# A graph network's edge passes: stored target one-hots for two blocks of three, a four-deep ring of slot rows, and sums of three blocks in three PSUM banks

## The chip, the core and the metric

The kernel runs on one core of a Trainium2 chip. The metric is the time of one execution on the device in microseconds (us), taken several times; the profile is one further execution. "PE" is TensorE, "DVE" VectorE, "ACT" ScalarE, "POOL" GpSimd, and "SP" SyncE, which here only issues DMAs.

## The reference, cut to what matters

Four graph layers follow each other over 12500 nodes of 32 features and 212500 edges sorted by target. Each gathers rows of the source nodes, weighs them, and adds them up by target. The passes that the change touches do this three times:

```python
def prop(v):                                   # layer 1, called twice
    return jax.ops.segment_sum(w_hat[:, None] * v[src], dst, num_segments=n)
...
msg_sum = jax.ops.segment_sum(x[src], dst, num_segments=n)   # layer 3
```

The weight of an edge is folded in as `ew` per edge and a factor per node. Layer 3 has no weight.

## The kernel before, in words

There are five passes over the edges, called `s` = 0 to 4: layer 0 (s = 0), the two propagations of layer 1 (s = 1 and 2), the attention of layer 2 (s = 3) and layer 3 (s = 4). The change touches s = 1, 2 and 4, here pass 1, pass 2 and pass 4.

In these passes about half of the edges are handled in one way and half in another, side by side.

- **Groups.** A group is 1024 edges. POOL gathers its rows with eight indirect DMAs (L790) into one of four slots of `arena`. DVE weighs them (`weigh_group`, L1636) and compares the next group's targets (L2105), PE multiplies (`multiply_group`, L1190, into `ps_agg`), and DVE adds the 80-wide window to the sums (`add_group`, L1662), which sets the slot free (L1656) for the gather of four groups later.
- **Blocks.** A block is 4096 edges, sorted in pass 0 by source into 49 buckets of 256 nodes with 128 places each. A block is worked through in eight batches `q` of seven or six buckets. For a batch SP brings the low source numbers from `lows_d` to all partitions (L688), DVE makes one-hots of the sources (`compare_sources`, L1888), and PE picks the rows by matmul (`pick`, L1304, or L1301 in pass 2). In passes 1 and 2 DVE weighs the picked rows (L1941, L1944) and they are split into three bf16 parts: ACT copies the high part (L969), DVE forms the rest (L1953), ACT the middle part (L973), and DVE the low part (L1958). In pass 4 ACT casts the picked rows at once (L1000). The parts of a batch lie in `slot_rows`, a ring of two. PE then multiplies them with the one-hots of the targets (`send`, L1321) and sums the 49 buckets of a block in one PSUM bank, `ps_t` (`ps_agg` in pass 2), and DVE adds the bank to the sums in `big` (`add_block`, L1912, or three steps at L1908 in pass 2).
- **Target one-hots.** In pass 1 DVE makes them (`compare_targets`, L1898, 128x256 for a bucket) and SP stores them to `targets_d` in DRAM. In pass 2 SP reads them back (L706). Pass 4 has 39 blocks, in 13 turns of three; the first of a turn (`e` in `RETURNED`) takes stored one-hots, and DVE makes those of the second and third.

The order of the work is written out by hand: each engine has its own program, and a step of it handles several batches at once, shifted against each other (DVE weighs batch q, and takes the rest of q-1 and the low part of q-2). `HIDDEN` and `HIDDEN4` tell with which batch a group is handled. A pass 1 or 2 loop body is one block with four groups; a pass 4 body is one turn of three blocks and four groups. Waits are on semaphores that count: `s_sent` batches multiplied by `send` (it starts at 2), `s_sbadd` blocks added, `s_free` slots set free. Pass 2 also carries other work for the table of the attention pass (`build_piece`, `next_pair` and what belongs to them), on PE, ACT and ACT's DMA queue.

Two waits stand in the middle of the change. In step q ACT waits for `s_sent` before it writes the ring's entry, so that batch q-2 has been multiplied:

```python
act.wait_ge(s_sent, at + 1)
act.wait_ge(s_wgh, at + 1)
```

And PE's `send` of a block's first batch waits until the block before has been taken out of the bank:

```python
pe.wait_ge(s_sbadd, (BEFORE[h] + e + 1) + i * UNIT[s])
```

Of the kernel before, what the change touches and what calls it, by code (L numbers as in the profile page):

```python
# [19 lines left out]
BF16 = mybir.dt.bfloat16  # L20
# [4 lines left out]
P = 128  # L25
# [36 lines left out]
RETURNED = (0,)  # L62
# [54 lines left out]
def gnn_kernel(nc, x, src, dst, et16, et86, ew, ew1, w0, comp0, w1, b1, w2, comp2, selfw,  # L117
# [14 lines left out]
    with ctx:  # L132
# [86 lines left out]
        slot_rows = [m[:, 640:976].bitcast(BF16).rearrange("p (k c) -> p k c", c=SPLIT) for m in (mem_a, mem_b)]  # L219
# [100 lines left out]
        block_sums = {1: ps_t, 2: ps_agg, 4: ps_t}  # L320
# [526 lines left out]
        def _(act):  # L847
# [100 lines left out]
            def pick_and_lay_out(s, h):  # L948
# [8 lines left out]
                def pick_weighed(i, f, first, last):  # L957
# [4 lines left out]
                    for q in range(NBATCH + (9 if last else 0)):  # L962
                        at = ((BEFORE[h] + f) * NBATCH + q) + i * NBATCH
                        if q < NBATCH:
                            n, b = BATCHES[q][1], q % 2
                            act.wait_ge(s_sent, at + 1)
                            act.wait_ge(s_wgh, at + 1)
                            carry_wait(act)
                            nc.scalar.copy(slot_rows[b][:, 0:n, 0:D], by_tile(weighed[b][:, 0:n * D])).then_inc(s_high, 1)  # L969
                        if goes(q - 1):  # L970
                            n, b = BATCHES[(q - 1) % NBATCH][1], (q - 1) % 2
                            act.wait_ge(s_rest, at)
                            nc.scalar.copy(slot_rows[b][:, 0:n, D:2 * D], by_tile(rest[b][:, 0:n * D])).then_inc(s_mid, 1)  # L973
# [20 lines left out]
                def pick_block(i, e):  # L994
                    for q, (b0, n) in enumerate(BATCHES):
                        b, at = q % 2, ((BEFORE[h] + e) * NBATCH + q) + i * (UNIT[s] * NBATCH)
                        act.wait_ge(s_got, at + 3)
                        act.wait_ge(s_sent, at + 1)
                        carry_wait(act)
                        nc.scalar.copy(slot_rows[b][:, 0:n, :], picked_rows(b)[:, 0:n, 0:SPLIT]).then_inc(s_slot, 1)  # L1000
                        if q in HIDDEN4[e]:
                            lay_out_next(s, i, HIDDEN4[e][q])
# [183 lines left out]
        def _(pe):  # L1186
# [94 lines left out]
            def pick_and_sum(s, h):  # L1281
# [25 lines left out]
                def send(i, e, q):  # L1307
                    b0, n = BATCHES[q]
                    if q == 0:
                        pe.wait_ge(s_sbadd, (BEFORE[h] + e + 1) + i * UNIT[s])  # L1310
                        carry_wait(pe)
# [8 lines left out]
                    for k in range(n):  # L1320
                        last = nc.tensor.matmul(block_sums[s][0:SPLIT, 0:W2], slot_rows[q % 2][:, k, :], to_oh[s][q % TO_RING[s]][:, k, :],  # L1321
                                                start=(b0 + k == 0), stop=(b0 + k == NBK - 1))
# [261 lines left out]
        def _(dve):  # L1584
# [287 lines left out]
            def pick_and_sum(s, h):  # L1872
# [28 lines left out]
                def add_block(i, e):  # L1901
# [9 lines left out]
                    else:  # L1911
                        op = V.tensor_tensor(into, into, ps_t[0:SPLIT, 0:W2], ALU.add)  # L1912
# [6 lines left out]
                def pick_weighed(i, f, first, last):  # L1919
# [9 lines left out]
                    for q in range(NBATCH + ((8 if s == 2 else 4) if last else 0)):  # L1929
# [20 lines left out]
                        if goes(q - 1):  # L1950
# [3 lines left out]
                                            slot_rows[b][:, 0:n, 0:D], ALU.subtract).then_inc(s_rest, 1)  # L1954
                        if goes(q - 2):
                            n, b = BATCHES[(q - 2) % NBATCH][1], q % 2
                            dve.wait_ge(s_mid, count(i, f, q, -1))
                            V.tensor_tensor(slot_rows[b][:, 0:n, 2 * D:SPLIT], by_tile(rest[b][:, 0:n * D]),  # L1958
                                            slot_rows[b][:, 0:n, D:2 * D], ALU.subtract).then_inc(s_slot, 1)
                        if q % NBATCH == 2 and (q >= NBATCH or not first):  # L1960
                            add_block(i, f + q // NBATCH - 1)
                        if q - 3 in HIDDEN[s]:
                            add_group(s, i, HIDDEN[s][q - 3], f)
                        if q == 1 and not first:
                            add_group(s, i, SLOTS - 1, f - 1)
                        if q - 1 in HIDDEN[s]:
                            weigh_group(s, i, HIDDEN[s][q - 1], f=f)
                        else:
                            dve.drain()
# [7 lines left out]
                def pick_turn(i, f, first, last):  # L1977
                    for e in range(UNIT[s]):
# [5 lines left out]
                        for q in range(NBATCH):  # L1984
# [6 lines left out]
                            if q == 0 and not (first and e == 0):  # L1991
                                add_block(i, n - 1)
# [474 lines left out]
```

## Time and profile before

| | us |
|---|---|
| median of 3 runs | 7698.59 (7696.14 to 7699.79) |
| the profiled execution's own time | 7688.82 |
| its span in the trace | 7687.0 |
| pass 0 with its preparations | to about 2250 |
| pass 1, first to last group weighed | 2336.9 to 3411.2 |
| pass 2, first to last block added | 3524.2 to 4703.8 |
| attention (pass 3) | about 4790 to 6870 |
| pass 4, first to last block added | 6959.2 to 7639.1 |

Over the span PE is busy for 63%, DVE for 59%, ACT for 31% and POOL for 68%. These are averages over passes with different limits, so each pass has to be read by itself. In rows of a timeline the first number is the start and the second the duration in us, and the brackets give the idle time of the engine before and what ended it; "issue" is time for which the trace shows no releaser. The "us" of a wait is a sum over the stretch that was asked for, followed by how often and by the longest.

### The profile page before, as it was taken

The numbers are of one execution on the slowest core, as the hardware profiler recorded it, in microseconds if no ns is written. First come the engines' busy times: TensorE is split into PE (matmuls) and PEld (weight loads), VectorE is DVE, ScalarE is ACT, GpSimd is POOL, SyncE is SP. The second block draws the span as 40 slices with busy tenths as digits, with TensorE's granted clock in tenths as the row PEclk, the third lists the DMA queues.
The fourth block names the chain that finished last, engine by engine and source line by source line (L and its number), as shares of the span: only waits on it lengthen the run. The fifth ranks groups of instructions, "written<-read, shape, count | busy, mean of one in ns | idle before, by whom it ended". The sixth has DMA issues, their size and how long they took to land. (4 is left out here: it accounts for less than half of the span.)

```text
span 7687.0 us, 150121 instructions
## 1 busy us (share of the span) xinstructions
PE 4849.7 (63%) x41375; PEld 4128.6 (54%) x41376; DVE 4540.0 (59%) x14144; ACT 2349.6 (31%) x7420; POOL 5231.6 (68%) x5417
## 2 busy tenths in 40 slices
PE   5333333333336767776777775777777777786777
PEld 2222222222225555565666665777777777775667
DVE  5555555557778888875555553444444444447776
ACT  4444444440002222213545454111112111123222
POOL 2777777777756777757666662777777777756663
PEclk8655555555556666668888786555555555558998
DMA  7000000000004444436888887222222222216554
GB/s 173 14 14 14 14 14 14 14 14 13 13 12 122 128 128 126 129 103 189 293 276 293 272 293 231 41 41 41 41 41 41 41 41 41 41 34 162 154 162 116
DMA packets 539741, 757.13 MB, mean 98 GB/s; under 512 B 226073, under 2 KB 382265, under 8 KB 539509
## 3 DMA queue, kind: packets, MB, share of 16 engines
q1 hardware_dynamic: 309893, 395.03, 16.9%
q0 software_dynamic: 173168, 146.14, 12.1%
q10 hardware_dynamic: 56448, 213.62, 7.2%
q14 instruction: 179, 1.47, 0.1%
q8 instruction: 53, 0.87, 0.0%
HBM read 424.12 MB, written 330.21 MB: 98 GB/s over the span
## 5 line engine op out<-in xcount | busy, mean ns | idle before, releaser
L790 POOL DMA_INDIRECT arena<-table,ibuf x3328 | 3150.1, 947 | 1241.7 <-issue 1125.7
L790 POOL DMA_INDIRECT arena<-nodes,ibuf x2080 | 2078.8, 999 | 1070.7 <-issue 616.8
L1190 PE MATMUL ps_agg<-mem_a,arena 128*32 128x80 f32 (+1 forms) x3744 | 470.0, 307 | 555.6 <-DVEq L1643 506.9
L1190 PE MATMUL ps_agg<-mem_b,arena 128*32 128x80 f32 (+1 forms) x3744 | 473.5, 308 | 511.4 <-DVEq L1643 498.0
L1190 PEld LDWEIGHTS ps_agg<-mem_a,arena 128*32 128x32 f32 (+1 forms) x3744 | 411.2, 155 | 615.2 <-DVEq L1643 524.8
L1190 PEld LDWEIGHTS ps_agg<-mem_b,arena 128*32 128x32 f32 (+1 forms) x3744 | 413.8, 156 | 560.8 <-DVEq L1643 521.4
L1459 PE MATMUL ps_agg<-tbuf,msg 128*64 128x80 f32 x2496 | 373.6, 344 | 330.6 <-DVE msg L2128 330.6
L1061 ACT ACTIVATE att<-score 128x8 f32<-128x8 f32 x208 | 43.3, 208 | 1649.5 <-DVE score L2119 1649.5
L1459 PEld LDWEIGHTS ps_agg<-tbuf,msg 128*64 128x64 f32 x2496 | 336.1, 227 | 351.7 <-DVE msg L2128 351.7
L913 ACT ACTIVATE tbuf<-O,tbuf 128x49 bf16<-128x49 bf16 x1664 | 448.7, 363 | 79.2 <-DVE H L1810 79.2
L1888 DVE TENSOR_SCALAR tbuf<-idx_a,pcol 128x768 bf16<-128x768 bf16 (+1 forms) x1040 | 397.3, 425 | 109.5 <-issue 53.6
L2111 DVE TENSOR_TENSOR msg<-arena,ps_z 128x256 f32<-128x256 f32 x208 | 87.7, 421 | 554.4 <-DMA arena<-table,ibuf 554.4
L1636 DVE TENSOR_TENSOR arena<-arena,ew_s 128x256 f32<-128x256 f32 x416 | 178.0, 428 | 370.7 <-DMA arena<-table,ibuf 290.3
L1662 DVE TENSOR_TENSOR big<-big,ps_agg 32x80 f32 (+1 forms) x468 | 108.2, 231 | 485.7 <-PE ps_agg L1190 419.0
L1454 PE MATMUL ps_wide<-yw,mem_b 80*128 80x33 f32 x1680 | 380.6, 404 | 1.2 <-ACT yw L1043 1.2
L1454 PE MATMUL ps_h<-yw,mem_b 80*128 80x33 f32 x1664 | 377.0, 403 | 0.0
L1454 PEld LDWEIGHTS ps_wide<-yw,mem_b 80*128 80x128 f32 x1680 | 366.4, 331 | 19.0 <-issue 17.7
L1454 PEld LDWEIGHTS ps_h<-yw,mem_b 80*128 80x128 f32 x1664 | 362.9, 331 | 17.8 <-issue 17.8
L969 ACT CAST mem_a<-msg 128x224 bf16<-128x224 f32 x208 | 74.5, 358 | 878.4 <-PE ps_t L1321 522.9
L904 ACT COPY ibuf<-idx_a 128x8 int32 x208 | 39.7, 196 | 926.7 <-DMA arena<-table,ibuf 924.8
L1212 PE MATMUL ps_wide<-O,not_before 128*128 128x392 bf16 x156 | 82.3, 527 | 359.8 <-DVE H L1810 359.8
L1446 PE MATMUL ps_wide<-ident,tbuf 128*80 128x128 f32 x1248 | 297.7, 421 | 0.0
(392 smaller groups left out, 12081.6 us busy)
## 6 DMA issues: line engine op xcount, KB each, us to landing
table<-tbuf ACTq DMA_DIRECT2D x294, 544.5 KB
idx_a<-lows_d SPq DMA_DIRECT2D x637, 192.0 KB
targets_d<-tbuf SPq DMA_DIRECT2D x182, 384.0 KB
H<-targets_d SPq DMA_DIRECT2D x182, 384.0 KB
arena<-table,ibuf POOLq DMA_INDIRECT x3328, 2.5
table<-tbuf ACTq DMA_DIRECT2D x98, 495.0 KB
O<-targets_d SPq DMA_DIRECT2D x91, 384.0 KB
arena<-nodes,ibuf POOLq DMA_INDIRECT x2080
```

Source lines behind the costliest of these rows:

```text
L790: nc.gpsimd.indirect_dma_start(out=INTO[s][:, k, c, 0:WIDTH[s]], out_offset=None, in_=TABLE[s], in_offset=bass.IndirectOffsetOnAxis(ap=ibu ...
L913: op = nc.scalar.mul(moved[:, j, 2 + part, :], by_bucket[:, j, :], of)
L969: nc.scalar.copy(slot_rows[b][:, 0:n, 0:D], by_tile(weighed[b][:, 0:n * D])).then_inc(s_high, 1)
L1190: last = nc.tensor.matmul(ps_agg[ROW0[s]:ROW0[s] + CHN[s], 0:WIN], narrow[:, k, c, 0:CHN[s]], onehots[b][:, c, :], start=(c == 0), stop=(c ...
L1212: nc.tensor.matmul(ps_wide[:, r, 0:392], not_before[:, :], bucket_oh[:, at], start=True, stop=False)
L1446: nc.tensor.transpose(ps_wide[0:WIN, c // 4, (c % 4) * P:(c % 4 + 1) * P], rows[:, c, :], ident[:, :])
L1454: last = nc.tensor.matmul(y_own[b][:, c, :], onehot_t[:, c, :], yw[:, :], start=True, stop=True)
L1459: last = nc.tensor.matmul(ps_agg[0:2 * D, 0:WIN], msg[:, c, :], onehots3[k][:, c, :], start=(c == 0), stop=(c == CH - 1))
L1636: V.tensor_tensor(rows, rows, by[:, of].unsqueeze(2).to_broadcast([P, CH, D]), ALU.mult)
L1662: V.tensor_tensor(into, into, ps_agg[r0:r1, 0:WIN], ALU.add)
L1888: op = V.tensor_scalar(from_oh[s][q % 2][:, a, 0:n * CAP], lows[q % RING][:, 0:n * CAP], pcol2[:, a:a + 1], None, ALU.is_equal)
L2111: V.tensor_tensor(msg[:, :, D:2 * D], gbuf[:, k, :, PAIR:PAIR + D], last_in_ps.unsqueeze(2).to_broadcast([P, CH, D]), ALU.mult)
```

## The change: what it does

There are four parts.

1. Pass 4: `RETURNED` becomes (0, 1). Of a turn's three blocks the first two take stored target one-hots and DVE makes those of the third alone. SP issues eight more transfers in a turn, and DVE 49 comparisons (L1898) less.
2. Passes 1, 2 and 4: `slot_rows` becomes a ring of four. ACT waits for batch q-4 to have been multiplied where it waited for batch q-2.
3. Pass 4: successive blocks are summed in `ps_t`, `ps_z` and `ps_h` by turns; PE's wait before a block's first batch asks for the block three before, and DVE adds a finished block at batch 2 of the next one instead of batch 0.
4. Pass 1: DVE weighs a group (odd steps) and adds it one step later (even steps), where it added it two steps later, right before it weighed the next; the add stands ahead of `add_block`, and steps without a group lose their closing drain. Pass 2 keeps its order.

```diff
-RETURNED = (0,)
+RETURNED = (0, 1)
...
+        more_rows = sb("more_rows", [P, 576])
+        slot_rows = [m.bitcast(BF16).rearrange("p (k c) -> p k c", c=SPLIT)
+                     for m in (mem_a[:, 640:976], mem_b[:, 640:928], more_rows[:, 0:288], more_rows[:, 288:576])]
...
-        block_sums = {1: ps_t, 2: ps_agg, 4: ps_t}
+        block_sums = {1: [ps_t], 2: [ps_agg], 4: [ps_t, ps_z, ps_h]}
...
-                            act.wait_ge(s_sent, at + 1)
+                            if (BEFORE[h] + f) * NBATCH + q > 1:
+                                act.wait_ge(s_sent, at - 1)
...
-                        act.wait_ge(s_sent, at + 1)
+                        act.wait_ge(s_sent, at - 1)
...
-                        pe.wait_ge(s_sbadd, (BEFORE[h] + e + 1) + i * UNIT[s])
+                        pe.wait_ge(s_sbadd, (BEFORE[h] + e + 2 - len(block_sums[s])) + i * UNIT[s])
...
+                        if s == 1:
+                            if q - 1 in HIDDEN[s]:
+                                weigh_group(s, i, HIDDEN[s][q - 1], f=f)
+                            if q - 2 in HIDDEN[s]:
+                                add_group(s, i, HIDDEN[s][q - 2], f)
+                            if q == 0 and not first:
+                                add_group(s, i, SLOTS - 1, f - 1)
                         if q % NBATCH == 2 and (q >= NBATCH or not first):
                             add_block(i, f + q // NBATCH - 1)
...
-                            if q == 0 and not (first and e == 0):
+                            if q == 2 and not (first and e == 0):
                                 add_block(i, n - 1)
```

Every other use of `slot_rows[b]` becomes `slot_rows[q % 4]` (or q-1, q-2), and `add_block` reads the block's own bank.

DVE's program in the loop of pass 1, an odd step and the even step behind it. Before, L1953 and L1958 end the split of a batch, L1662 is the add of a group, L1636 the weighing and L2105 the comparison for the next group:

```order
L1953 TENSOR_TENSOR msg<-msg,mem_a 128x192
L1958 TENSOR_TENSOR mem_b<-msg,mem_b 128x6x32
...
L1662 TENSOR_TENSOR big<-big,ps_agg 32x80
...
L1636 TENSOR_TENSOR arena<-arena,ew_s 128x8x32
L2105 ISA
L2105 TENSOR_TENSOR mem_a<-iota,drel 128x640
L1888 TENSOR_SCALAR tbuf<-idx_a,pcol 128x768 x2
```

Of the changed kernel, in the same place (its lines are L1956, L1961, L1639, L2116, L1891, L1665 for the same six; the add stands at the end):

```order
L1956 TENSOR_TENSOR msg<-msg,more_rows 128x192
L1961 TENSOR_TENSOR mem_b<-msg,mem_b 128x6x32
L1639 REGISTER_ALU
L1639 TENSOR_TENSOR arena<-arena,ew_s 128x8x32
L2116 ISA
L2116 TENSOR_TENSOR mem_a<-iota,drel 128x640
L1891 TENSOR_SCALAR tbuf<-idx_a,pcol 128x768 x2
...
L1901 TENSOR_SCALAR tbuf<-iota,at_f 128x256 x6
...
L1665 TENSOR_TENSOR big<-big,ps_agg 32x80
```

The add has moved from ahead of the weighing to the end of the next step.

DVE's program of pass 4 around the start of a turn's second block. Before, the target one-hots (L1898) are made into `O` and the finished block is added from `ps_t` at once:

```order
L1888 TENSOR_SCALAR tbuf<-idx_a,pcol 128x768 x2
L1898 TENSOR_SCALAR O<-iota,at_f 128x256 x7
L1902 ISA
L1902 TENSOR_LOAD block_i
L1912 ISA
L1912 TENSOR_TENSOR big<-big,ps_t 96x256
L2105 ISA
L2105 TENSOR_TENSOR mem_a<-iota,drel 128x640
```

Of the changed kernel, from the start of a turn on (L1891 compares sources, L1915 adds the block before, which lies in a bank of its own):

```order
L1891 TENSOR_SCALAR tbuf<-idx_a,pcol 128x768 x2
L1905 ISA
L1905 TENSOR_LOAD block_i
L1915 ISA
L1915 TENSOR_TENSOR big<-big,ps_h 96x256
L1635 ISA
L2116 ISA
L2116 TENSOR_TENSOR mem_b<-iota,drel 128x640
```

In the first two blocks of a turn the rows of L1901 (the former L1898) are gone, and the add comes behind three comparisons of sources.

## Rows read from the trace of the kernel before

**Rows 1.** Busy time by engine (x instructions), PE clock, DMA share, GB/s, by pass

```profile
2330.00:3420.00 1090.00, 780.44 (x6015) 642.93 (x6015) 926.58 (x2885) 241.03 (x1044) 825.04 (x827) 0.66 0.45 127
3480.00:4710.00 1230.00, 919.72 (x13928) 785.15 (x13928) 657.07 (x1992) 602.70 (x1844) 796.84 (x822) 0.81 0.85 274
6959.00:7640.00 681.00, 499.75 (x6386) 436.70 (x6383) 533.65 (x2052) 201.20 (x353) 414.85 (x391) 0.95 0.58 155
```

**Rows 2.** Waits in pass 1, 2400 to 3400: us in total, times, longest

```profile
POOL arena L790 <- issue: 223.5, 733, 0.3
POOL arena L790 <- DVEq L1656: 10.1, 33, 0.3
```

**Rows 3.** Timeline of pass 1, an even and an odd step

```profile
2852.89 2.34 PE L1190 MATMUL ps_agg<-mem_b,arena 128*32 128x80 f32 x16
...
2854.52 0.35 DVE L1958 TENSOR_TENSOR mem_a<-msg,mem_a 128x192 bf16<-128x192 f32 x1
2855.11 0.76 DVE L1888 TENSOR_SCALAR tbuf<-idx_a,pcol 128x768 bf16<-128x768 bf16 x2 [0.24 <-issue]
...
2859.15 0.23 DVE L1662 TENSOR_TENSOR big<-big,ps_agg 32x80 f32 x1
2859.64 0.42 DVE L1636 TENSOR_TENSOR arena<-arena,ew_s 128x256 f32<-128x256 f32 x1 [0.27 <-issue]
```

**Rows 4.** Timeline of pass 4, an add that waits for PE

```profile
7219.24 1.29 PE L1190 MATMUL ps_agg<-mem_a,arena 128*32 128x80 f32 x16
...
7220.76 0.23 DVE L1662 TENSOR_TENSOR big<-big,ps_agg 32x80 f32 x1 [2.47 <-PE ps_agg L1190]
```

**Rows 5.** Waits in pass 2, 3600 to 4600

```profile
ACT mem_a L969 <- PE ps_agg L1321: 243.2, 81, 7.1
...
DVE msg L1953 <- ACT mem_a L969: 129.3, 44, 3.8
...
DVE msg L1953 <- ACT mem_b L969: 50.7, 51, 2.8
```

**Rows 6.** L1908, three for each block of pass 2: ns, first and last start

```profile
L1908 DVE TENSOR_TENSOR big<-big,ps_agg x78: 415/419/424, 3524.2 to 4703.8; 32x256 f32 x78
```

**Rows 7.** Timeline of pass 2, one step

```profile
4002.36 2.34 PE L1190 MATMUL ps_agg<-mem_b,arena 128*32 128x80 f32 x16 [0.30 <-issue]
4004.63 1.27 PE L1321 MATMUL ps_agg<-H,mem_a 128*96 128x256 bf16 x6
...
4006.04 0.35 ACT L969 CAST mem_a<-msg 128x192 bf16<-128x192 f32 x1 [3.32 <-PE ps_agg L1321]
...
4006.43 0.36 DVE L1953 TENSOR_TENSOR msg<-msg,mem_a 128x192 f32<-128x192 f32 x1 [3.28 <-ACT mem_a L969]
...
4007.40 0.24 DVE L1662 TENSOR_TENSOR big<-big,ps_agg 32x80 f32 x1 [0.35 <-issue]
```

**Rows 8.** L1912, one for each block of pass 4

```profile
L1912 DVE TENSOR_TENSOR big<-big,ps_t x39: 401/410/420, 6959.2 to 7639.2; 96x256 f32 x39
```

**Rows 9.** Stretches of pass 4: two busy moments, and a block with made one-hots

```profile
7208.00:7210.00 2.00, 0.43 (x4) 0.17 (x2) 0.13 (x1) 0.03 (x1) 1.39 (x3) 1.00 0.99 281
...
7280.00:7282.00 2.00, 1.01 (x19) 0.88 (x18) 1.11 (x5) 1.12 (x3) 1.56 (x2) 1.00 1.01 374
...
7228.26:7246.82 18.56, 13.98 (x184) 11.87 (x181) 17.49 (x72) 5.68 (x10) 13.86 (x12) 1.00 0.40 98
```

**Rows 10.** Timeline of DVE at the start of a turn of pass 4

```profile
7209.87 0.89 DVE L1888 TENSOR_SCALAR tbuf<-idx_a,pcol 128x768 bf16<-128x768 bf16 x2 [2.42 <-issue]
7213.75 0.42 DVE L1912 TENSOR_TENSOR big<-big,ps_t 96x256 f32 x1 [3.00 <-issue]
```

**Rows 11.** Instruction queue, packets and MB: 7000 to 7600, then 2400 to 3400

```profile
q14 instruction: 53, 0.43, 0.2%
...
q14 instruction: 3, 0.02, 0.0%
```

**Rows 12.** PE's wait for stored one-hots in pass 4, 7000 to 7600

```profile
PE ps_t L1321 <- DMA O<-targets_d: 5.9, 10, 0.8
```

More of the change, by code:

```diff
@@ L1320, in send @@
                     for k in range(n):
-                        last = nc.tensor.matmul(block_sums[s][0:SPLIT, 0:W2], slot_rows[q % 2][:, k, :], to_oh[s][q % TO_RING[s]][:, k, :],
+                        last = nc.tensor.matmul(block_sums[s][e % len(block_sums[s])][0:SPLIT, 0:W2], slot_rows[q % 4][:, k, :], to_oh[s][q % TO_RING[s]][:, k, :],
                                                 start=(b0 + k == 0), stop=(b0 + k == NBK - 1))
@@ L1911, in add_block @@
                     else:
-                        op = V.tensor_tensor(into, into, ps_t[0:SPLIT, 0:W2], ALU.add)
+                        op = V.tensor_tensor(into, into, block_sums[s][e % len(block_sums[s])][0:SPLIT, 0:W2], ALU.add)
                     op.then_inc(s_sbadd, 1)
@@ L1957, in pick_weighed @@
                             dve.wait_ge(s_mid, count(i, f, q, -1))
-                            V.tensor_tensor(slot_rows[b][:, 0:n, 2 * D:SPLIT], by_tile(rest[b][:, 0:n * D]),
-                                            slot_rows[b][:, 0:n, D:2 * D], ALU.subtract).then_inc(s_slot, 1)
+                            V.tensor_tensor(slot_rows[(q - 2) % 4][:, 0:n, 2 * D:SPLIT], by_tile(rest[b][:, 0:n * D]),
+                                            slot_rows[(q - 2) % 4][:, 0:n, D:2 * D], ALU.subtract).then_inc(s_slot, 1)
+                        if s == 1:
[5 more added lines that the diff above has]
+                                add_group(s, i, SLOTS - 1, f - 1)
                         if q % NBATCH == 2 and (q >= NBATCH or not first):
                             add_block(i, f + q // NBATCH - 1)
[L1962 to L1969, printed above, removed]
+                        if s == 2:
+                            if q - 3 in HIDDEN[s]:
+                                add_group(s, i, HIDDEN[s][q - 3], f)
+                            if q == 1 and not first:
+                                add_group(s, i, SLOTS - 1, f - 1)
+                            if q - 1 in HIDDEN[s]:
+                                weigh_group(s, i, HIDDEN[s][q - 1], f=f)
+                            else:
+                                dve.drain()
                         if s == 2 and q % 4 == 2 and (q >= 6 or not first) and q < NBATCH + 4:
```

9 lines of the change are left out of this document (4 added, 5 removed).

## The prediction

> **What bounds the kernel now.** I split the span by pass first, because its averages mix stages with different limits [rows 1]. Pass 1 is tight twice: DVE is busy for 926.58 of 1090 us, and POOL for 825.04, in 827 gathers of 0.998 us. The waits of pass 1 add what the busy time hides [rows 2]: POOL pauses about 0.30 us ahead of every gather and never longer than 0.3 us, so it never waits for a slot. 32 gathers for a block at 0.998 + 0.30 give 41.5 us, and pass 1 takes about that for a block. No wait of DVE there is for another engine or a DMA either. Both are full, DVE in its own order, and freeing slots earlier can bring POOL nothing.
>
> Pass 2 takes (4703.8 - 3524.2) / 25 = 47.2 us for a block [rows 6], and nothing is full: DVE 53%, PE 75%, ACT 49%, DMA 0.85 [rows 1]. Its waits form a loop [rows 5]: ACT waits for PE's `send` (243.2 us in 1000), DVE for ACT's high part (129.3 + 50.7), and PE's next batch for DVE. One step shows it link by link [rows 7]: `send` ends at 4005.90, ACT starts the high part at 4006.04, DVE goes on at 4006.43 after 3.28 us.
>
> Pass 4 takes (7639.1 - 6959.2) / 38 = 17.89 us for a block, 53.7 us for a turn [rows 8]. A block whose one-hots are made takes 18.56 us with DVE busy for 17.49 of it [rows 9]: DVE bounds it. At a turn's start DVE stands still twice with no releaser, 2.42 and 3.00 us [rows 10], while PE has nothing to do.
>
> **Part 1, stored one-hots for the second block (pass 4).** It takes 49 comparisons from a DVE that is the bound there, and puts 49 x 64 KB = 3.21 MB on the DMA engines. What the block costs then is the DMA's: its one-hots and 1.61 MB of source numbers are 4.82 MB. I price this in two ways. By bytes: in the five stretches of 2 us from 7200 to 7300 in which the share was 0.92 or more, the rate was 281 to 374 GB/s, 321 on average [rows 9]; 4.82 MB take 15.0 us. By share: a turn has 0.58 x 53.7 = 31.1 us of DMA time [rows 1], a made block 0.40 x 18.56 = 7.4 [rows 9], so the returned block has 31.1 - 2 x 7.4 = 16.3 us. I take 15.7. Two such blocks in a row are 31.4 us, less the two batches that SP fetches ahead while the third block leaves the DMA idle (0.79 MB, 2.5 us); with the made block, which stays at DVE's 18.56, the turn is 31.4 - 2.5 + 18.6 = 47.5 us. The saving is 6.2 x 13 = 81 us. The ends: no turn can be shorter than its 32 gathers, 41.5 us by pass 1's pace (157 us saved); and if the engines get no fuller than pass 2's 0.85, the block by share costs 16.3 / 0.87 = 18.8 us, the turn 53.7, and nothing is saved. I take no loss here from the two fetched blocks alone; what could make one is the last rival.
>
> **The standing still at the turn's start (pass 4).** The instruction queue moved 53 packets of 8 KB in 600 us of pass 4 and 3 in 1000 us of pass 1 [rows 11]: about four for each turn. DVE's loop of pass 4 is the longest of the three (336 instructions in the built program, against 283 and 299 in passes 1 and 2), and the change cuts it to 287. I expect the two pauses to vanish. They are not added to the 81 us, since the DMA goes on fetching during them and it is the DMA that sets the new turn.
>
> The Trainium skill ("Runtime: NRT & Kernel Launch", Instruction fetch mechanics) says that a taken branch to a target outside a window of two pages of 256 instructions has to fetch before it goes on. By that rule the pauses of rows 10 are the loop's jump back, and where a loop lies matters as much as its length: loops shift in the changed program, and one that comes to span three pages would pay at each turn. The trace agrees as far as the four packets go.
>
> **Part 3, three PSUM banks (pass 4).** PE no longer waits for `add_block`, 0.5 us after a block's end in the made ones. In the returned blocks the DMA hides it; in the made one DVE is the bound and still does the same add. I count 0.
>
> **Part 2, the ring of four.** In pass 1 DVE has no wait for ACT at all, and in pass 4 ACT hardly waits for `send`: 0. In pass 2 it opens the loop. DVE's waits for the high part are 180 us in 1000, 8.5 us for a block [rows 5]. Not all comes back. In the step of rows 7 DVE would take up L1953 about 2.7 us earlier, but its add of the group then waits for PE's L1190, which ends at 4004.70, so the add starts near 4004.9 instead of 4007.40: 2.5 us for DVE. PE, which is back to back behind it, gains only the 0.9 us or so that it waited for ACT. A gain between 0.9 and 2.5 of 3.28 is 27 to 76%, 2.3 to 6.5 us for a block. What comes next is near: POOL's 32 gathers take 32 x (0.969 + 0.30) = 40.6 us [rows 1], and DMA goes from 0.85 to 0.91 when a block falls to 44. I take 3.0 us, close to the low end, because PE is the slower partner: block 44.2, and 3.0 x 25 = 75 us. The ends are 0, since a wait is loosened and nothing is added, and 6.2 x 25 = 155, at 41.0.
>
> The Trainium skill ("DMA: Bandwidth & Descriptors", Specifications) gives about 358 GB/s as a core's share of HBM. Pass 2 moves 274 GB/s of it [rows 1], so by that rule its block could not fall under 36 us, which changes nothing; a returned block of pass 4 would take 13.5 us and the turn 43.3, a saving of 135 us. The trace reaches that rate in one of the five stretches and lies under it in four.
>
> **Part 4, the new order in pass 1.** It moves the add of a group to the end of an even step, and there PE has only just multiplied. L1190 ends at 2855.23, DVE's L1958 at 2854.87 [rows 3]; over the 104 groups the middle value of that lag is 0.31 us. DVE starts 0.23 us after PE has ended [rows 4]. So the add begins about 0.54 us after L1958. Summing the pauses of two steps from rows 3: before, 0.24 (L1958 to L1888), 0.18 on average (to the add; 0.12 in rows 3, 0.25 elsewhere) and 0.27 (add to L1636); after, 0.54, 0.27 and 0.12. The pair grows by 0.24 us, for 104 groups 25 us, and all of it is DVE's path, which is the bound. POOL has slots in hand and doesn't notice. The lost drains are in that sum already (the 0.12). The ends are 0, if PE is quicker at the place, and 104 x 0.35 = 36.
>
> **The sum.** 25 - 75 - 81 = -131 us. The profiled execution took 7688.82 us, which becomes 7558; the median of the runs is 9.8 us above it, so I predict 7568 us.
>
> **Rivals.**
> - *The DMA engines are the bound wherever the change wants more from them.* Pass 4 saves nothing (turn 53.7) and pass 2 half of my figure, 37: 7698.6 + 25 - 37 = 7687. For it: a share of 0.99 with only 281 GB/s [rows 9], and two returned blocks in a row. Against: pass 2 runs at 0.85 for 1200 us with no engine waiting much for a DMA. A milder form, pass 4 saving 30 and pass 2 75, gives 7619.
> - *Everything flows.* The loop of pass 2 opens to 41.5 us (142 saved), pass 4 comes to 44.5 (120): 7698.6 + 25 - 262 = 7462. For it: PE's and DVE's own work is under 39 us in a block of pass 2. Against: three resources at over 90% rarely meet without losses.
> - *Only pass 4 or only pass 2 gains.* 7643 or 7649.
> - *The pauses move to pass 1.* If its loop comes to lie badly, 5.4 us in each of 24 turns are 130 us: 7568 + 130 = 7698, no change. Against: the loop got shorter (279 instructions) and moved by four.
> - *Slower: the order of transfers in pass 4.* SP issues a target batch three steps ahead of its use. If with both queues full a batch lands 8 us after its issue, a step is 8 / 3 = 2.7 us, a returned block 21.3, the turn 21.3 x 2 - 2.5 + 18.6 = 58.7 and pass 4 65 us longer; with pass 1's 25 and pass 2's 37 saved the kernel takes 7752. It decides from a landing of about 7 us. For it: PE waits for a stored batch already, with one returned block in a turn [rows 12]. Against: only 10 such waits in 600 us, 5.9 us in all, none over 0.8.
>
> **How the numbers follow.** The forecast with its own range, 7500 to 7620, has 0.60; everything flows 0.12; one pass alone, or the milder form of the DMA bound, 0.15; the full DMA bound 0.06; the pauses in pass 1 0.03; slower 0.04. A measurement of this kernel tells about 0.2%, 15 us, from no change. So faster has 0.91 (the full DMA bound gives 12 us and I share it between faster and same), same 0.04, slower 0.05. The range leaves out most of "everything flows" below and the DMA bound above: 7470 to 7655.
>
> **What would show it.** L1908's counterpart spaced by about 44 us in pass 2, and DVE's waits for ACT's high part gone from the list; a turn of 47 to 48 us in pass 4 with a DMA share near 0.8, PE waiting for stored one-hots in the first two blocks and for DVE in the third; few packets on the instruction queue; in pass 1 DVE waiting for L1190 ahead of the add about 100 times. The prediction is wrong if pass 2's block stays above 46 us, if the turn stays above 52, or if pass 1 grows by more than 36 us.

## The result, and the profile after

The changed kernel takes 7580.21 us (median of 4 runs, 7574.09 to 7583.85), the kernel before took 7697.36 us on the same chip (4 runs): ratio 0.9848, 95% interval 0.9831 to 0.9865. 7568 us was predicted, with a range of 7470 to 7655. The profiled execution of the changed kernel took 7583.85 us, its span is 7582.1 us.

The total is near the forecast. The parts are less so, and the runs below show that the gain in pass 4 came for other reasons than the forecast's. A pass is measured here from its first source comparison (L1888 before, L1891 after) to the next pass's first; pass 3 from its first L1459 (L1462). In us:

| | before | after | difference | forecast |
|---|---|---|---|---|
| pass 0 | 2329.4 | 2340.0 | +10.6 | 0 |
| pass 1 | 1151.8 | 1165.4 | +13.6 | +25 |
| pass 2 | 1319.0 | 1261.2 | -57.8 | -75 |
| pass 3 | 2141.6 | 2141.7 | 0 | 0 |
| pass 4 to the end | 745.2 | 673.8 | -71.4 | -81 |

Busy time by pass in the changed kernel, the columns as in [rows 1]:

```profile
2340.00:3440.00 1100.00, 767.58 (x6002) 630.81 (x6003) 922.92 (x2884) 265.49 (x1040) 809.05 (x828) 0.69 0.42 126
3505.00:4675.00 1170.00, 879.47 (x13919) 760.29 (x13923) 657.86 (x1988) 609.63 (x1843) 801.15 (x821) 0.84 0.87 287
6931.00:7536.00 605.00, 478.10 (x6335) 415.31 (x6335) 415.17 (x1413) 200.32 (x352) 401.50 (x388) 0.99 0.77 239
```

DVE's work in pass 4 fell from 533.65 to 415.17 us and the DMA share rose from 0.58 to 0.77; passes 1 and 2 do the same work as before, pass 2 in less time.

The adds of blocks, which answer to [rows 6] and [rows 8] (count, ns of one, first and last start). They give 44.9 us for a block of pass 2 (before 47.2) and 47.9 us for a turn of pass 4 (before 53.7):

```profile
L1911 DVE TENSOR_TENSOR big<-big,ps_agg x78: 415/419/423, 3549.3 to 4671.8; 32x256 f32 x78
L1915 DVE TENSOR_TENSOR big<-big,ps_z x13: 403/407/413, 6949.4 to 7524.4; 96x256 f32 x13
```

The waits in pass 2 of the changed kernel, 3600 to 4600, against [rows 5]. ACT's wait for `send` is gone from the top of the list. DVE's wait for ACT's high part, 180 us before, is still 114 us, though the forecast had it vanish:

```profile
DVE msg L1956 <- ACT mem_a L972: 63.6, 39, 2.6
...
DVE msg L1956 <- ACT mem_b L972: 44.7, 41, 2.2
...
DVE msg L1956 <- ACT more_rows L972: 5.3, 8, 2.2
```

The timeline of ACT in one step of pass 2 shows what lies ahead of the high part (L972) there: the pieces of the attention's table, which ACT copies and sends between two high parts.

```profile
4014.45 0.47 ACT L1118 COPY tbuf<-ps_z 128x330 f32<-128x330 f32 x1
4015.09 0.90 ACTq L1123 DMA_DIRECT2D table<-tbuf  x2
4016.18 0.35 ACT L972 CAST mem_b<-msg 128x192 bf16<-128x192 f32 x1 [1.26 <-issue]
4016.44 0.35 ACT L976 CAST mem_a<-msg 128x192 bf16<-128x192 f32 x1
```

DVE's next step, in the same stretch, starts 0.93 us late for it:

```profile
4015.28 0.36 DVE L1947 TENSOR_TENSOR msg<-ps_wide,slot_ew 128x192 f32<-128x192 f32 x1 [0.24 <-issue]
4016.56 0.36 DVE L1956 TENSOR_TENSOR msg<-msg,mem_b 128x192 f32<-128x192 f32 x1 [0.93 <-ACT mem_b L972]
```

In pass 4, 7000 to 7500, DVE and PE now wait for DMAs; PE did so in [rows 12] for 5.9 us in 600:

```profile
DVE tbuf L1891 <- DMA idx_a<-lows_d: 45.2, 57, 2.4
...
PE ps_z L1324 <- DMA O<-targets_d: 14.9, 25, 1.3
PE ps_t L1324 <- DMA O<-targets_d: 14.8, 31, 1.9
```

The stops at a turn's start [rows 10] are gone, and the instruction queue moved 5 packets from 7000 to 7600, against 53 in [rows 11]:

```profile
q14 instruction: 5, 0.04, 0.0%
```

### The profile page after: what moved, and what is told of

Its sections match the earlier page's. It is cut to its first block and busy times, and to the rows that moved or that the text cites. A ratio compares the mean times of both kernels' runs of the same rounds, so it can differ in the third digit from the quotient of the medians.

```text
span 7582.1 us, 149745 instructions
## 1 busy us (share of the span) xinstructions
PE 4782.4 (63%) x41375; PEld 4075.7 (54%) x41376; DVE 4420.6 (58%) x13507; ACT 2382.5 (31%) x7420; POOL 5221.1 (69%) x5417
## 5 line engine op out<-in xcount | busy, mean ns | idle before, releaser
L792 POOL DMA_INDIRECT arena<-nodes,ibuf x2080 | 2058.1, 989 | 980.3 <-issue 633.7
L1193 PE MATMUL ps_agg<-mem_b,arena 128*32 128x80 f32 (+1 forms) x3744 | 454.5, 300 | 515.5 <-DVEq L1646 501.6
L1193 PEld LDWEIGHTS ps_agg<-mem_b,arena 128*32 128x32 f32 (+1 forms) x3744 | 398.1, 151 | 565.1 <-DVEq L1646 525.1
L1462 PE MATMUL ps_agg<-tbuf,msg 128*64 128x80 f32 x2496 | 373.5, 344 | 329.7 <-DVE msg L2139 329.7
L1462 PEld LDWEIGHTS ps_agg<-tbuf,msg 128*64 128x64 f32 x2496 | 336.0, 227 | 350.8 <-DVE msg L2139 350.8
L1891 DVE TENSOR_SCALAR tbuf<-idx_a,pcol 128x768 bf16<-128x768 bf16 (+1 forms) x1040 | 402.5, 430 | 136.7 <-DMA idx_a<-lows_d 56.6
L1665 DVE TENSOR_TENSOR big<-big,ps_agg 32x80 f32 (+1 forms) x468 | 108.4, 232 | 577.1 <-PE ps_agg L1193 516.6
L1639 DVE TENSOR_TENSOR arena<-arena,ew_s 128x256 f32<-128x256 f32 x416 | 176.8, 425 | 372.5 <-DMA arena<-table,ibuf 308.0
L2173 DVE TENSOR_TENSOR big<-big,ps_agg 64x80 f32 x208 | 47.9, 230 | 401.3 <-PE ps_agg L1462 401.3
```

Of the source, the lines that this page charges most:

```text
L792: nc.gpsimd.indirect_dma_start(out=INTO[s][:, k, c, 0:WIDTH[s]], out_offset=None, in_=TABLE[s], in_offset=bass.IndirectOffsetOnAxis(ap=ibu ...
L1193: last = nc.tensor.matmul(ps_agg[ROW0[s]:ROW0[s] + CHN[s], 0:WIN], narrow[:, k, c, 0:CHN[s]], onehots[b][:, c, :], start=(c == 0), stop=(c ...
L1462: last = nc.tensor.matmul(ps_agg[0:2 * D, 0:WIN], msg[:, c, :], onehots3[k][:, c, :], start=(c == 0), stop=(c == CH - 1))
L1639: V.tensor_tensor(rows, rows, by[:, of].unsqueeze(2).to_broadcast([P, CH, D]), ALU.mult)
L1665: V.tensor_tensor(into, into, ps_agg[r0:r1, 0:WIN], ALU.add)
L1891: op = V.tensor_scalar(from_oh[s][q % 2][:, a, 0:n * CAP], lows[q % RING][:, 0:n * CAP], pcol2[:, a:a + 1], None, ALU.is_equal)
```

## The experiments

All passes were read in each profile in the same way. Ratios are to the kernel before in the same series. The first eight kernels ran on chips on which the kernel before takes 7691 and 7693 us.

| kernel | ratio (95%) | pass 0 | pass 1 | pass 2 | pass 4 | a turn |
|---|---|---|---|---|---|---|
| before | 1 | 2329.4 | 1151.8 | 1319.0 | 745.2 | 53.7 |
| changed | 0.9848 (0.9831-0.9865) | 2340.0 | 1165.4 | 1261.2 | 673.8 | 47.9 |
| a_ring | 0.9929 (0.9916-0.9943) | 2329.8 | 1154.8 | 1274.3 | 747.5 | |
| b_stored | 0.9932 (0.9918-0.9945) | 2331.8 | 1151.7 | 1315.2 | 687.9 | 49.2 |
| c_old_order | 0.9841 (0.9827-0.9854) | 2329.1 | 1150.3 | 1264.9 | 680.4 | 48.1 |
| d_one_bank | 0.9874 (0.9859-0.9889) | 2330.9 | 1158.7 | 1267.1 | 693.6 | 49.7 |
| p_pad | 0.9938 (0.9924-0.9951) | 2333.4 | 1154.2 | 1319.2 | 694.4 | 49.8 |
| q_pad | 0.9946 (0.9932-0.9960) | 2331.0 | 1164.5 | 1266.5 | 747.2 | 54.1 |
| i_add_q0 | 0.9869 (0.9854-0.9885) | 2330.2 | 1165.4 | 1264.5 | 692.7 | 49.4 |
| e_half | 0.9756 (0.9743-0.9769) | 2328.0 | 1162.2 | 1231.4 | 631.0 | 44.6 |

"A turn" is the mean distance of the adds of blocks, three blocks on, over all of pass 4; which adds are taken shifts it by up to 0.5 us. Passes with the same code differ between two profiles by up to 13 us (pass 4 by up to 7: the changed kernel and c_old_order); where it can be done, several profiles are compared below.

**a_ring: the ring of four alone.**

```
 in before:
+more_rows = sb("more_rows", [P, 576])
+slot_rows = [... four ..., indexed q % 4]
-act.wait_ge(s_sent, at + 1)
+act.wait_ge(s_sent, at - 1)
```

> The kernel before with the ring of four slot_rows alone (its PSUM banks, stored one-hots and the order in pass 1 as before). Theory (the parts add up, and the ring is the whole gain of pass 2): pass 2 takes 1261 us, as in the changed kernel, instead of 1319, with DVE waiting for ACT's L972 about 40 + 40 times in 1000 us; passes 1 and 4 stay at 1152 and 742 us; in all 58 us below before, ratio 0.9925. Rival (the new order or the banks had a hand in pass 2): pass 2 saves under 45 us. On pass 0: if more_rows, which moves the tiles allocated behind it, made pass 0 10 us longer, pass 1's first source comparison starts near 2340 us here; if that was a difference between two executions, it lies anywhere from 2329 to 2341.

Pass 2 took 1274.3 us, 45 less than before, passes 1 and 4 stayed (3 and 2 us more). The ratio is worth 55 us, with 10 either way. Six profiles with the ring lie from 1261.2 to 1274.3 in pass 2 (mean 1266.4), three without it from 1315.2 to 1319.2 (1317.8): the ring brings 51 us, and it brings all of pass 2's gain. Pass 0 was not made longer by it; nine of ten profiles lie between 2328.0 and 2333.4, and 2340.0 is that one execution's.

**b_stored: the stored one-hots for the second block alone.**

```
-RETURNED = (0,)
+RETURNED = (0, 1)
```

> The kernel before with RETURNED = (0, 1) alone: in pass 4 two blocks of three take stored one-hots, with the ring of two and one PSUM bank. Theory (the stored one-hots are the whole gain of pass 4, and the banks nothing): a turn of 47.9 us, pass 4 at 671 us, passes 1 and 2 at 1152 and 1319; in all 71 us below before, ratio 0.991; the two stops of DVE at a turn's start gone, since its loop is 287 instructions here too. Rival (without the banks and the ring PE's wait for the add of the block before costs in the returned blocks): turn of 49 to 50 us, 20 us less saved.

Pass 4 took 687.9 us, 57 less than before, and a turn 49.2 us. So 14 us of the gain (8 against c_old_order, whose pass 4 has the changed kernel's code) needed something else of the change, as the rival said. The loop of pass 4 has the changed kernel's 287 instructions here too, and its stops are gone; what of the 57 us is due to that was open, and is asked by p_pad.

**c_old_order: the changed kernel with pass 1's old order.**

```
 in after, pick_weighed, for s == 1 as for s == 2:
+if q % NBATCH == 2 ...: add_block(...)
+if q - 3 in HIDDEN[s]: add_group(...)
+if q - 1 in HIDDEN[s]: weigh_group(...)
```

> The changed kernel with the old order of DVE's work in pass 1 (add of the block and of the group before the weighing). Theory (the new order alone costs pass 1 its 13.6 us): blocks at 41.4 us instead of 41.8, pass 1 at 1152 us, the kernel 13 us faster than the changed one, near 7567. Rival 1 (my forecast's price of 25 us was right and the ring gave 11 back in pass 1): pass 1 at 1141 us, near 7555. Rival 2 (the ring or the moved tiles cost pass 1 the time): pass 1 stays at 1165 us.

Pass 1 took 1150.3 us. Over all profiles, the five with the old order have a mean of 1152.6 us (1150.3 to 1154.8) and the five with the new order 1163.2 us (1158.7 to 1165.4): the new order costs 10.7 us. The theory stands for the order's cost. In the whole time the kernel can't be told from the changed one: 0.9841 against 0.9848, both within 0.0017.

The idle time of DVE in 2400 to 3400, first with the old order (c_old_order), then with the new one (the changed kernel), shows where that is:

```profile
DVE msg L1947 <- issue: 32.6, 186, 0.2
DVE arena L1639 <- issue: 28.0, 94, 0.6
DVE tbuf L1891 <- issue: 27.1, 96, 0.4
DVE big L1665 <- issue: 12.0, 47, 0.5
```

```profile
DVE tbuf L1891 <- issue: 32.1, 95, 0.4
DVE big L1665 <- PE ps_agg L1193: 27.7, 62, 0.6
DVE big L1915 <- issue: 20.7, 23, 1.1
```

At the pieces that the forecast summed (L1891, the group's add L1665, L1639), 67.1 us became 59.8 and a few short ones: nothing was lost there. New is 0.9 us ahead of each block's add L1915, which stood idle for nothing in the old order. In that place its register load comes right behind the group's add and drain; that this is the cause is argued from the code and wasn't tested.

**d_one_bank: the changed kernel with one PSUM bank.**

```
-block_sums = {..., 4: [ps_t, ps_z, ps_h]}      -if q == 2 and ...: add_block(i, n - 1)
+block_sums = {..., 4: [ps_t]}                  +if q == 0 and ...: add_block(i, n - 1)
```

> The changed kernel with one PSUM bank in pass 4 and the add of a block back at q == 0. Theory (the banks are worth nothing, PE's wait being hidden by the DMA in the returned blocks and by DVE in the made one): turn 47.9 us, the kernel within 5 us of the changed one. Rival (each block's start waits for the add, 0.5 us and more, 39 times): 20 us slower, turn 49.4.

The rival was right: 0.9874 against 0.9848 is 20 us, with 17 either way, pass 4 took 693.6 us, a turn 49.7. In 7000 to 7500 both engines wait at the block's end, PE for the add and DVE for the last matmul:

```profile
PE ps_t L1324 <- DVE big L1915: 19.9, 20, 1.4
DVE big L1915 <- PE ps_t L1324: 18.1, 21, 1.6
```

**i_add_q0: three banks, but the add at q == 0.** Which of the two waits costs?

```
-if q == 2 and not (first and e == 0): add_block(i, n - 1)
+if q == 0 and not (first and e == 0): add_block(i, n - 1)
```

> The changed kernel with its three PSUM banks in pass 4 but the add of a block back at q == 0, where DVE has to wait for PE's last matmul of the block. With one bank and the add at q == 0 pass 4 took 17 to 20 us more than with both changes. Theory 1 (DVE's wait for PE at the add, 1.8 us a turn, holds up the comparisons behind it): pass 4 stays near 690 us, 15 to 20 us slower than the changed kernel. Theory 2 (PE's wait for the add, 2.0 us a turn, is what costs): pass 4 near 674 us, as the changed kernel.

PE's wait is gone, DVE's is as long as with one bank (12.8 + 5.7 us), and pass 4 took 692.7 us, as with one bank:

```profile
DVE big L1915 <- PE ps_t L1324: 12.8, 10, 1.8
...
DVE big L1915 <- PE ps_h L1324: 5.7, 11, 0.5
```

Theory 1 holds. The banks by themselves are worth nothing that these profiles show (692.7 against 693.6 us). What they allow is worth 12 to 19 us: DVE may do the add two steps later, when PE has long finished, and no longer stands before its comparisons. (With one bank the late add would hold up PE's next block; that wasn't tried.)

**p_pad: the kernel before, its loop of pass 4 in another place.**

```
 in before, ahead of DVE's loop of pass 4, run once:
+for _ in range(60):
+    dve.drain()
```

> The kernel before with 60 drains of DVE ahead of its loop of pass 4 (run once, about 3 us), so that this loop of 336 instructions starts at 3 instead of 199 in a page of 256 of the built program and spans two pages instead of three. Theory (the two stops of 2.42 and 3.00 us in each turn are the loop's place, not its length): the stops vanish, the instruction queue moves under 10 packets in 7000:7600 instead of 53; the turn is made shorter only in so far as DVE bounds it there: up to 5.4 us for each of 13 turns, and as PE and DMA have slack after them I expect 2 to 4 us, 25 to 50 us in all less the 3 us. Rival (it is the length, 336 against 287): the stops stay and the kernel is 3 us slower.

Sixty instructions that do nothing make the kernel 48 us faster (7642.27 against 7693.13 is 51 us in the medians; ratio 0.9938 with 0.0014 either way). Pass 4 took 694.4 us, 50.8 less, a turn 49.8 us. The start of a turn, as in [rows 10]:

```profile
7204.58 0.42 DVE L1912 TENSOR_TENSOR big<-big,ps_t 96x256 f32 x1 [0.53 <-PE ps_t L1321]
7205.30 1.42 DVE L1888 TENSOR_SCALAR tbuf<-idx_a,pcol 128x768 bf16<-128x768 bf16 x4 [0.30 <-issue]
```

And the instruction queue in 7000 to 7600, 53 packets in [rows 11]:

```profile
q14 instruction: 9, 0.07, 0.0%
```

The stops came from the place of the loop: moving it is enough to be rid of them, at its full length. What they cost is more than the means of the table tell. The 49.8 us hold the drains themselves, over which DVE stands idle for 3.36 us, once. The 53.7 us hold the turns at both ends of the pass, which lie outside the loop and took 49.8 and 50.2 us. The ten turns with a jump back took 54.6 us on average before and 49.3 in p_pad, so the stops cost 5.3 us in each. Their own length in these ten turns is 3.6 to 5.4 us, 4.4 on average; rows 10 show the longest. What comes on top stands behind the stop: the granted clock was 0.66 in 7210 to 7212 and 0.50, the lower of the two levels (1.2 GHz), in 7212 to 7216, with PE idle from 7212 to 7214. The same twelve matmuls, first before and then in p_pad, where the clock stayed at 1.00:

```profile
7210.81 1.14 PE L1304 MATMUL ps_wide<-arena,tbuf 128*128 128x96 bf16 x12 [2.38 <-DVE tbuf L1888]
```

```profile
7204.18 0.67 PE L1304 MATMUL ps_wide<-arena,tbuf 128*128 128x96 bf16 x12
```

Over 7000 to 7500 the granted clock was 0.94 before and 0.99 in p_pad. That the clock makes up all of the 0.9 us between 4.4 and 5.3 is not shown.

**q_pad: the changed kernel, its loop of pass 4 in a bad place.**

```
 in after, ahead of DVE's loop of pass 4, run once:
+for _ in range(70):
+    dve.drain()
```

> The changed kernel with 70 drains of DVE ahead of its loop of pass 4 (run once, about 3.5 us), so that this loop of 287 instructions starts at 204 instead of 134 in a page of 256 and, if the true start lies 22 to 51 instructions further on than in the built program, spans three pages. Theory (place decides): the two stops are back at each turn's start, four 8 KB packets for each turn (about 40 in 500 us), and pass 4 is 20 to 60 us longer than the changed kernel's. Rival (length decides): no stops, 3.5 us slower.

The stops are back, in one piece, and with them 53 packets in 7000 to 7600 and a turn of 54.1 us. Pass 4 took 747.2 us, as long as before the change and 73 us more than in the changed kernel, where 20 to 60 were expected. The ten turns with a jump back took 54.9 us on average against 47.9, so a stop of 4.9 to 5.9 us costs 7.0; the granted clock was again 0.94, against 1.00 in the changed kernel. DVE's wait at the turn's start, PE's wait that follows from it, and the instruction queue:

```profile
7234.09 1.63 DVE L1891 TENSOR_SCALAR tbuf<-idx_a,pcol 128x768 bf16<-128x768 bf16 x4 [5.30 <-issue]
```

```profile
PE ps_wide L1307 <- DVE tbuf L1891: 72.3, 63, 5.7
```

```profile
q14 instruction: 53, 0.43, 0.2%
```

The DMA doesn't cover the stops: SP fetches at most four batches ahead, and then the DMA stands still as well. In this stop, from 7228.8 to 7234.1, its share (the last number but one) was 0.89 and then 0.15:

```profile
7230.00:7232.00 2.00, 0.00 (x0) 0.00 (x0) 0.00 (x0) 0.00 (x0) 1.50 (x2) 1.00 0.89 303
7232.00:7234.00 2.00, 0.00 (x0) 0.00 (x0) 0.00 (x0) 0.00 (x0) 1.39 (x3) 0.70 0.15 37
```

Its share was 0.71 in 7000 to 7500, against 0.79 in the changed kernel.

The Trainium skill ("Runtime: NRT & Kernel Launch", Instruction fetch mechanics) has the rule of the two pages of 256 instructions. These two runs agree with it as far as the place decides and not the length. Where the page borders lie is a fit: pages are counted in the built program, and the true start must lie 22 to 51 instructions further on for all loops seen here to fit. By the bare count q_pad's loop (287 instructions from place 204 of a page) would span two pages, and pass 1's (283 from 243), which doesn't stop, three. The loops seen before q_pad allow 17 to 56; both ends of the narrower range come from q_pad itself.

**e_half: less to fetch.** From the second turn on, three columns of each stored transfer instead of six or seven.

```
-sp.dma_start(to_oh[...][:, 0:BATCHES[q][1], :], kept_rows(i, ..., q))
+sp.dma_start(to_oh[...][:, 0:3, :], kept_rows(i, ..., q)[:, 0:3 * W2])
```

> The changed kernel with each stored one-hot transfer of passes 2 and 4 carrying 3 of its 6 or 7 columns (after the first turn of each; the other columns keep those of an earlier block, so the sums of these passes are left wrong). A block's one-hots are 1.57 instead of 3.21 MB. Theory for pass 4 (the DMA engines set the returned blocks): turn from 47.9 to 44 or 45 us, pass 4 40 to 50 us shorter, DVE's waits for idx_a<-lows_d and PE's for targets_d gone. Theory for pass 2 (ACT's order sets it now, not the DMA): block stays within 0.5 us of 44.9, DVE's waits for L972 stay. Rival for pass 2 (DMA at 0.9 sets it): block falls by 1.5 us or more, 40 us in the pass. Rival for pass 4 (PE and DVE in turn set the block): turn stays above 47.

Pass 4: 42.8 us shorter, a turn 44.6 us: the DMA sets the returned blocks, as expected, though DVE still waits for idx_a<-lows_d (13.7 us in 500). Pass 2: 1231.4 us against 1266.4, the mean of the six profiles with the ring. That is 35 us; the block fell from 44.9 to 43.8 us, between the 0.5 of the theory and the 1.5 of the rival. Pass 2's busy time, and the waits for the high part that stayed:

```profile
3505.00:4635.00 1130.00, 854.41 (x13668) 738.93 (x13665) 645.70 (x1959) 608.73 (x1838) 790.19 (x809) 0.85 0.81 260
```

```profile
DVE msg L1962 <- ACT mem_a L978: 53.3, 43, 2.2
DVE msg L1962 <- ACT mem_b L978: 50.3, 42, 2.2
```

So the DMA is a limit of pass 2. The waits for ACT's high part (104 us in these two rows) are hardly shorter; whether ACT's order is a second limit is what j_defer and y_defer ask.

**k_one_stored and j_defer.** Two open questions: what the stored one-hots are worth once the loop lies well and the add comes late, and whether ACT's DMA issues in pass 2 can be moved behind the high part.

```
 both: from c_old_order
 k: RETURNED = (0,), and 60 drains ahead of DVE's loop of pass 4
 j: in ACT's pick_weighed, s == 2
-next_piece(act, q % 4, turned, built, build_piece)
+next_piece(act, q % 4, ..., build_piece if q % 4 == 3 else lay_out_piece)
+... and behind the next step's L976: next_piece(act, q % 4 - 1, ..., send_piece)
```

> The changed kernel with the old order in pass 1, RETURNED back at (0,) and 60 drains of DVE ahead of its loop of pass 4, so that this loop (336 instructions again) spans two pages: everything of the change but the stored one-hots of the second block and the new order. The same kernel with RETURNED = (0, 1) (ratio 0.9841 to before) took 680 us for pass 4; the kernel before, with only the place of the loop changed, 694 us. Theory (the stored one-hots of the second block are worth little by themselves; what pass 4 gained is the loop's place, 51 us, and the later add, 15 to 19 us): pass 4 at 676 to 684 us, ratio 0.983 to 0.986. Rival (the stored one-hots carry part of it, as forecast, the DMA having room): pass 4 at 690 us or more, ratio above 0.986.

> The changed kernel with the old order in pass 1, and in pass 2 ACT issues the two DMAs of a finished table piece (0.9 us, and 0.2 to 0.4 us until its next copy) only after the next step's L972 and L976, for three pieces of four. Theory (DVE's remaining 108 us of waits for L972 in 1000 us come from ACT being late behind these issues): those waits fall under 60 us, pass 2 is 10 to 30 us shorter than 1265 us, ratio to before 0.980 to 0.983. Rival 1 (the table pieces that leave later hold up ACT's next copies, which already wait 44 us for DMA table<-tbuf): no gain or a loss of up to 20 us. Rival 2 (PE's wait for H L1891 and DVE's own order set the block): waits for L972 fall and pass 2 stays within 5 us.

These ran on another chip, and there the kernel before takes 10751.4 us. DVE and POOL are busy as long as in the kernel before elsewhere (4582 and 5187 us in k, against 4540 and 5232), PE for 5277 against 4850 us, at a mean granted clock of 0.592 against 0.644; the rest of the 3000 us more is waiting, a good part of it for events that the trace names "remote". Ratios: k 0.9882 (0.9847-0.9917), j 0.9891 (0.9859-0.9922). Pass 4: k 1039.1, j 1020.3. Pass 2: k 1960.8, j 1958.6.

**x_one_defer and y_defer.** The same questions again, with j's edit in both, so that pass 4 alone differs between the two.

```
 x: y with RETURNED = (0,), and 60 drains ahead of DVE's loop of pass 4
 y: j_defer again
```

> The changed kernel with the old order in pass 1, the later DMA issues of ACT in pass 2, RETURNED back at (0,) and 60 drains of DVE ahead of its loop of pass 4, so that this loop (336 instructions again) spans two pages. Its mate with RETURNED = (0, 1) and no drains is y_defer, on the same chip; a first look at both questions on another chip, on which the kernel before takes 10751 us instead of 7690 because its DMAs land late, can't answer them for this one. Theory (the stored one-hots of the second block are worth little by themselves; what pass 4 gained is the loop's place and the later add): pass 4 at 676 to 684 us, within 6 us of the mate's. Rival (they carry part of it, as forecast): pass 4 at 690 us or more, 10 us or more above the mate's.

> The changed kernel with the old order in pass 1, and in pass 2 ACT issues the two DMAs of a finished table piece only after the next step's L972 and L976, for three pieces of four. Theory (DVE's remaining 108 us of waits for L972 in 1000 us come from ACT being late behind these issues): those waits fall under 60 us, pass 2 is 10 to 30 us shorter than 1265 us, ratio to before 0.980 to 0.983. Rival 1 (the pieces that leave later hold up ACT's next copies, which already wait 44 us for DMA table<-tbuf): no gain or a loss of up to 20 us. Rival 2 (PE's wait for H L1891 and DVE's own order set the block): the waits for L972 fall and pass 2 stays within 5 us.

A chip of the same kind again: the kernel before took 10662.5 us. x 0.9897 (0.9882-0.9911), y 0.9919 (0.9899-0.9938). Pass 4: x 1041.7, y 1021.6. Two lines on what this chip is waiting for, DVE in 3000 to 4500 (pass 1) of k_one_stored, which had no idle time at all ahead of it in 2400 to 3400 of c_old_order, and the gathers of the table, as long as ever (947 ns in c_old_order) but with 2705 us of idle time ahead of them instead of 1240:

```profile
DVE tbuf L1901 <- remote: 417.8, 95, 5.1
```

```profile
L792 POOL DMA_INDIRECT arena<-table,ibuf x3328 | 3155.7, 948 | 2705.0 <-issue 1088.5
```

By the code L1901 waits there for the landing of one-hots stored two batches before, which is what the expectation of x_one_defer means by DMAs that land late. The landings that the traces time don't bear it out: the stores of `nodes` land a median of 3.0 us after their issue on both kinds of chip, those of `table` that SP issues 4.3.

On these two chips the second block's stored one-hots shorten pass 4 by 19 and 20 us, and in the whole time nothing of it is seen, because pass 3 alone, whose code is the same, lies between 2959 and 3025 us there. That doesn't carry over to a chip on which other waits decide. Of j's edit they say nothing: DVE waits for the high part for only 8 to 12 us in 1000 there, with the edit and without. Both questions stay open for the faster chips. There is only the comparison of p_pad with b_stored, with the add early: 6.5 us in pass 4, of which the drains of p_pad are 3.4, and 49.3 against 49.2 us in the ten turns with a jump back, which is nothing that can be told from zero.

## Why the prediction was right, and where it was wrong

**The instruction stops (pass 4): seen, explained, and priced at nothing.** The forecast expected the stops to vanish, and gave the reason: the loop spans fewer pages. Then it said that they "are not added to the 81 us, since the DMA goes on fetching during them and it is the DMA that sets the new turn". That is the step that failed. p_pad shows that they cost 51 us of the kernel before (54 with the drains taken off), and q_pad that a changed kernel that keeps them gains nothing in pass 4. The DMA runs ahead by four batches only: some 3 us into q_pad's stop it stands still too. The 5.4 us that the forecast took from rows 10 for a stop is the longest of ten; the mean is 4.4.

**The stored one-hots (-81, pass 4 measured -71.4).** The new turn came out at 47.9 us, 47.5 was forecast, but by two errors. From one block's first `send` to the next, on average over the turns in the loop, the two returned blocks of the changed kernel take 14.8 and 16.2 us, 31.0 together, where the forecast had 31.4 - 2.5 = 28.9. The made block takes 16.9 and not 18.56. The 18.56 was read from a turn's second block; the third takes 16.7 in p_pad, and in the kernel before the stops hid that (20.8). And the turn that 47.5 was subtracted from, 53.7 us, holds the stops. Without them the turns in the loop take 49.3 us, and the stored one-hots bring 0.1 of that. In pass 4 the 71.4 us are made up so: place and length of the loop 54, stored one-hots 3, later add 14, each with some 7 us of scatter; in a turn of the loop 5.3, 0.1 and 1.3 us, in all the 6.7 from 54.6 to 47.9. The parts hold in this order only. The later add was measured with the one-hots stored, and its gain stands in the turn's second block (18.2 us in b_stored, 16.2 in the changed kernel); what it would bring a block with made one-hots is open.

**Three PSUM banks (0): right for the banks, wrong for the add.** The forecast looked at PE's wait for the add, and i_add_q0 shows no gain from ending this wait. It missed the other side of the same edit: with the add at q == 0 DVE waits 1.8 us in a turn for PE, and moving it to q == 2 gives 12 to 19 us.

**The ring (-75, measured -51).** The mechanism is right and all of pass 2's gain is the ring's. The term of 3.0 us for a block is what was too large: 51 us over 25 blocks are 2.1. It was read from one step, of which between 27 and 76% was to come back. What holds the block now is shown in part. e_half shows that the DMA does, at a share of 0.84, where the forecast let it reach 0.91. In the step shown above ACT, which works in order, copies and sends a table piece between two high parts, and the forecast had no line of such work; ACT was 49% busy, and a mean of half doesn't show that the half lies in the way. That it costs the pass time is argued from these waits and wasn't shown by a run. PE waits as well, for DVE's source one-hots (L1891), 133 us in 1000, and before the change it was 117.

**The new order in pass 1 (+25, measured +10.7).** The two steps of the sum, L1958 to L1888 and the group's add, did not grow. DVE stood idle for 0.30 us ahead of a group's add on average (28 us in 95 adds), not for 0.54: PE is done earlier than the old trace let expect. The loss is 0.9 us ahead of each of 26 block adds, 23 us, and the steps of the sum gave about 8 of it back (67.1 to 59.8 in 1000 us). That leaves 15 where 10.7 were measured, which is within the scatter of these profiles. The forecast moved the block's add behind the group's and priced nothing for it.

**Pass 0 (+10.6)** is hardly an effect of the change: the nine other profiles don't show it, six of them with the ring. It may be part of why the profiled execution gained 105 us and the medians 117; the other executions have no trace.

**A slip in the bounds.** "Nothing is saved" in pass 4 was worked with a share of 0.87 where the text says 0.85. With 0.85 the block is 19.2 us and the turn 54.5, a small loss. The forecast itself doesn't use it.

The forecast was thus right by errors that cancelled: too much for the ring and the stored one-hots, too much loss for the order, a late add and a chance of code placement counted at nothing. The same edits, with DVE's program 70 instructions longer in an unlucky place, took 7647 us (q_pad).

## What to carry over

When an engine stands still at a loop's start without a releaser and the instruction queue moves packets there, test the place before the work: shift the loop by some tens of drains ahead of it. Do that to the kernel before as well, or a change that merely moves code will be credited with the difference. And price an edit from both sides of each semaphore: a buffer or a bank that frees one engine often frees the other to do its part later, and that can be all of its worth.

## What the runs showed that was not expected

- Sixty drains made a kernel of 7693 us 51 us faster, and seventy made one of about 7577 us 70 us slower (0.9946 against 0.9848, with 0.0017 either way). No length of the loop is safe by itself: 287 instructions stopped, 336 did not.
- Two chips ran the same program 39 to 40% slower (10662 and 10751 us instead of 7691), with DVE and POOL busy for the same time as elsewhere. What makes these chips wait wasn't found. A ratio taken there weighs the parts of a kernel in another way: the same second block that gives 3 us in pass 4 on one kind of chip, with the add early, gives 19 to 20 on the other, with the add late.
- A stop of DVE costs more than its length. Turns with stops of 4.4 us on average were 5.3 us longer, and turns with stops of 5.6 us were 7.0 us longer; PE stood idle in the stop that was looked at and its granted clock was 0.50 behind it, where the same twelve matmuls took 1.14 us instead of 0.67.
- An add that waits for nothing in one place had an idle time of 0.9 us ahead of it in another, behind an add and its drain, with the same instructions.
